# Causal attention with one exp over a pair of key blocks instead of one exp for each

## The reference

```python
x = x + _layernorm(_L0_attn_ref(_layernorm(x), Wq, bq, Wk, bk, Wv, bv, Wo, bo))
x = x + _layernorm(_L0_ffn_ref(_layernorm(x), w_up, w_down))
...
scores = jnp.einsum('bqhd,bkhd->bhqk', Q, K)
causal = jnp.tril(jnp.ones((S, S), bool))
scores = jnp.where(causal[None, None], scores, -jnp.inf)
attn = jax.nn.softmax(scores.astype(jnp.float32), axis=-1).astype(X.dtype)
out = jnp.einsum('bhqk,bkhd->bqhd', attn, V).reshape(B, S, D)
return out @ Wo.T + bo
```

## Time and profile before

| | |
|---|---|
| two runs, median | 6665.75 us (6662.55 and 6668.95) |
| the profiled execution, its own time | 6643.92 us |
| its span on core 7, first to last instruction | 6642.4 us |
| spans of the eight cores | 6576.3 to 6642.4 us |
| PE busy | 3147.3 us (47 %), 10388 matmuls |
| ACT busy | 907.2 us (14 %) |
| DVE busy | 1902.5 us (29 %) |
| mean granted PE clock, core 7 | 0.704 of full speed |

### The profile page before, as it was taken

How to read it: one execution, slowest core, us unless ns; L and a number is a source line. 1 busy time by engine, 2 the same in 40 slices (tenths; PEclk the granted TensorE clock), 3 DMA queues, 4 the chain that set the end, 5 groups by cost and what they waited for, 6 DMA issues and landing times.

```text
span 6642.4 us, 35789 instructions; the slowest of 8 cores (6576.3 to 6642.4 us)
## 1 busy us (share of the span) xinstructions
PE 3147.3 (47%) x10388; PEld 1086.2 (16%) x10388; DVE 1902.5 (29%) x2752; ACT 907.2 (14%) x1249; POOL 380.4 (6%) x716
## 2 busy tenths in 40 slices
PE   0000744444744445554446544443857636566276
PEld 0000311111211111211112110111323212222132
DVE  1153121111111111211111311113456265263562
ACT  1100001112011111022111012220011111011110
POOL 0001100000100000100001000001000000000000
PEclk9999855555755556655557655555878868788688
DMA  5677210000200001200001100013133334433343
GB/s 95 101 253 209 44 38 31 32 31 32 45 25 32 31 32 34 60 16 24 29 32 42 41 32 32 19 73 127 51 103 104 95 120 108 152 101 96 108 118 98
DMA packets 358610, 472.21 MB, mean 71 GB/s; under 512 B 161553, under 2 KB 317201, under 8 KB 337681
## 3 DMA queue, kind: packets, MB, share of 16 engines
q0 software_dynamic: 69136, 251.74, 13.6%
q1 hardware_dynamic: 289282, 218.19, 12.3%
HBM read 385.92 MB, written 83.89 MB: 71 GB/s over the span
## 4 chain that ended last, share of the span: by engine, by line
PE 40%; DVE 17%; DMA 15%; ACT 13%; issue 6%; DVEq 4%; POOL 2%; SPq 2%; ACTq 0%; POOLq 0%
ACT pt L643 7%; PE psB L660 6%; PE psB L1033 6%; PE psB L1159 5%; PE psA L634 4%; PE psB L664 4%; PE psB L435 3%; PE psB L473 3%; PE psB L559 3%; DMA xt<-x 3%; DMA wqch<-wdnt 3%; DMA wqch<-wupt 2%; PE psB L776 2%; DVE tq_bf L387 2%; PE psB L505 2%
## 5 line engine op out<-in xcount | busy, mean ns | idle before, releaser
L660 PE MATMUL psB<-pt,ones_bf 128*128 128x512 bf16 x640 | 374.1, 585 | 789.6 <-DVEq L91 431.7
L1033 PE MATMUL psB<-wsl_f,qfm_ar 128*128 128x512 bf16 x2048 | 476.4, 397 | 434.2 <-DMA qfm_ar<-qtile 434.2
L1159 PE MATMUL psB<-wsl_f,qfm_ar 128*128 128x512 bf16 x2048 | 503.6, 412 | 268.8 <-DMA qfm_ar<-qtile 221.4
L643 ACT ACTIVATE pt<-psA,negC 128x512 bf16<-128x512 f32 x640 | 439.7, 687 | 1134.7 <-PE psA L634 1132.7
L650 DVE TENSOR_TENSOR pt<-pt,strip 128x512 bf16<-128x512 bf16 x256 | 109.0, 426 | 1474.0 <-ACT pt L643 1474.0
L634 PE MATMUL psA<-qh,kg 128*128 128x512 bf16 x640 | 397.9, 622 | 83.9 <-ACTq L91 83.9
L664 PE MATMUL psB<-pt,vg 128*128 128x512 bf16 x640 | 404.3, 632 | 0.0
L585 PE MATMUL psB<-sq_t,ones_f 128*128 128x512 f32 x128 | 87.3, 770 | 565.7 <-DVEq L91 565.7
L559 PE MATMUL psB<-y_fm,wsl 128*128 128x512 bf16 x1024 | 288.0, 444 | 134.8 <-DVEq L91 134.8
L1033 PEld LDWEIGHTS psB<-wsl_f,qfm_ar 128*128 128x128 bf16 x2048 | 206.6, 101 | 704.0 <-issue 484.4
L435 PE MATMUL psB<-y_fm,wsl 128*128 128x512 bf16 x1024 | 231.0, 390 | 180.9 <-DVEq L91 124.5
(11 more groups left out here) (153 smaller groups left out, 3013.2 us busy)
## 6 DMA issues: line engine op xcount, KB each, us to landing
wsl_f<-tup_sp SPq DMA_DIRECT2D x512, 128.0 KB, 2.8
wsl_f<-tdn_sp SPq DMA_DIRECT2D x512, 128.0 KB, 2.9
wch<-wupt POOLq DMA_DIRECT2D x16, 2048.0 KB, 8.7
wch<-wdnt POOLq DMA_DIRECT2D x32, 1024.0 KB, 5.4
wqch<-wupt POOLq DMA_DIRECT2D x32, 1024.0 KB, 5.7
wqch<-wdnt POOLq DMA_DIRECT2D x32, 1024.0 KB, 5.9
xt<-x SPq DMA_DIRECT2D x16, 1024.0 KB, 12.4
tup_sp<-tq_bf POOLq DMA_DIRECT2D x128, 128.0 KB, 2.2
```

The costliest lines, as they stand in the source:

```text
L643: exp_done[(hq, k)] = p.op("scalar", lambda e, sl=sl: e.activation(out=p4(sl), in_=S4[sl][:, :], func=ACT.Exp, bias=negC[:], scale=1.0), i ...
L660: p.op("tensor", lambda e, sl=sl, k=k, nk=nk: e.matmul(PS[5][:, :], ones_bf[:, :], p4(sl), start=(k == 0), stop=(k == nk - 1)))
L1033: t_mm = p.op("tensor", lambda e, par=par, c=c, t=t, j=j: e.matmul(PS[par][:, :], q1fm[:, c * 512 + t * 128: c * 512 + (t + 1) * 128], wsl ...
L1159: t_mm = p.op("tensor", lambda e, par=par, c=c, t=t, s=s: e.matmul(PS[par][:, :], q2fm[:, c * 512 + t * 128: c * 512 + (t + 1) * 128], wsl ...
```

## The change

Key blocks are handled in pairs: `u` counts pairs, `ns = nk // 2` is their number, `sb = u % 2` the buffer. For a pair PE issues two score matmuls (after: L632, L636) into the two halves of one 1024-column slot of `psA`; only the second raises the semaphore. ACT computes one exp over the 1024 columns (L645). In a masked pair DVE applies two masks, one to each half (L655), and signals once. PE then issues two row-sum matmuls (L666, L669) and two value matmuls (L672, L677). The keys of `exp_done`, `mask_done` and `pv_mm` are pairs now, so the waits two slots back go by pairs. As `nk - 4` is even, a pair is masked in both halves or in none. The line numbers of the code behind the loop are 13 higher.

```diff
-                for k in range(nk):
-                    sl = k % 4
-                    if k >= 4:
-                        p.wait("tensor", SA, exp_done[(hq, k - 4)])
-                    elif hq >= 1:
-                        p.wait("tensor", SA, exp_done[(hq - 1, nk_prev - 4 + k)])
...
-                    t_smm = p.op("tensor", lambda e, sl=sl, hl=hl, k=k, qsl=qsl: e.matmul(
-                        S4[sl][:, :],
-                        kg[:, hl * S + k * 128: hl * S + (k + 1) * 128],
+                for u in range(ns):
+                    sb = u % 2
+                    if u >= 2:
+                        p.wait("tensor", SA, exp_done[(hq, u - 2)])
+                    elif hq >= 1 and ns_prev - 2 + sb >= 0:
+                        p.wait("tensor", SA, exp_done[(hq - 1, ns_prev - 2 + sb)])
...
+                    p.op("tensor", lambda e, sb=sb, hl=hl, u=u, qsl=qsl: e.matmul(
+                        S2[sb][:, 0:512],
+                        kg[:, hl * S + (2 * u) * 128: hl * S + (2 * u + 1) * 128],
+                        qsl, start=True, stop=True))
+                    t_smm = p.op("tensor", lambda e, sb=sb, hl=hl, u=u, qsl=qsl: e.matmul(
+                        S2[sb][:, 512:1024],
+                        kg[:, hl * S + (2 * u + 1) * 128: hl * S + (2 * u + 2) * 128],
                         qsl, start=True, stop=True), inc=ST)
                     p.wait("scalar", ST, t_smm)
...
-                    exp_done[(hq, k)] = p.op("scalar", lambda e, sl=sl: e.activation(
-                        out=p4(sl), in_=S4[sl][:, :], func=ACT.Exp,
+                    exp_done[(hq, u)] = p.op("scalar", lambda e, sb=sb: e.activation(
+                        out=p_t[sb][:], in_=S2[sb][:, 0:1024], func=ACT.Exp,
                         bias=negC[:], scale=1.0), inc=SA)
...
+                        for half in range(2):
+                            kc = 2 * u + half
+                            if kc >= nk - 4:
+                                m = kc - 4 * qb
+                                p.op("vector", lambda e, sb=sb, m=m, half=half: e.tensor_tensor(
+                                    out=p_t[sb][:, half * 512:(half + 1) * 512],
+                                    in0=p_t[sb][:, half * 512:(half + 1) * 512],
+                                    in1=strip[:, 384 - 128 * m: 896 - 128 * m],
+                                    op=ALU.mult))
+                        mask_done[(hq, u)] = p.sig("vector", SV)
+                    p.wait("tensor", SA, exp_done[(hq, u)])
                     if diag:
-                        p.wait("tensor", SV, mask_done[(hq, k)])
-                    if k == 0 and qb == 0:
+                        p.wait("tensor", SV, mask_done[(hq, u)])
+                    if u == 0 and qb == 0:
                         p.wait("tensor", SV, cap_v)
```

More of the change, by code:

```diff
@@ L655, in build_core @@
-                    p.wait("tensor", SA, exp_done[(hq, k)])
+                        p.wait("vector", SA, exp_done[(hq, u)])
+                        for half in range(2):
[7 more added lines that the diff above has]
+                                    op=ALU.mult))
@@ L663, in build_core @@
-                    pv_mm[(hq, k)] = p.op("tensor",
-                        lambda e, sl=sl, k=k, qpar=qpar, hl=hl, nk=nk: e.matmul(
+                    p.op("tensor", lambda e, sb=sb, u=u: e.matmul(
+                        PS[5][:, :], ones_bf[:, :], p_t[sb][:, 0:512],
+                        start=(u == 0), stop=False))
+                    p.op("tensor", lambda e, sb=sb, u=u, ns=ns: e.matmul(
+                        PS[5][:, :], ones_bf[:, :], p_t[sb][:, 512:1024],
+                        start=False, stop=(u == ns - 1)))
@@ L665, in build_core @@
+                    p.op("tensor", lambda e, sb=sb, u=u, qpar=qpar, hl=hl: e.matmul(
+                        PS[6 + qpar][:, :],
+                        vg[:, (2 * u) * 512 + hl * 128: (2 * u) * 512 + (hl + 1) * 128],
+                        p_t[sb][:, 0:512], start=(u == 0), stop=False))
+                    pv_mm[(hq, u)] = p.op("tensor",
+                        lambda e, sb=sb, u=u, qpar=qpar, hl=hl, ns=ns: e.matmul(
                             PS[6 + qpar][:, :],
-                            vg[:, k * 512 + hl * 128: k * 512 + (hl + 1) * 128],
@@ L667, in build_core @@
-                            p4(sl), start=(k == 0), stop=(k == nk - 1)),
+                            vg[:, (2 * u + 1) * 512 + hl * 128: (2 * u + 1) * 512 + (hl + 1) * 128],
+                            p_t[sb][:, 512:1024], start=False, stop=(u == ns - 1)),
                         inc=ST)
-                p.wait("scalar", ST, pv_mm[(hq, nk - 1)])
+                p.wait("scalar", ST, pv_mm[(hq, ns - 1)])
                 if hq >= 2:
```

29 lines of the change are left out of this document (9 added, 20 removed).

## The result

The changed kernel took 6206.98 us (median of 11 runs, 6198 to 6253), the kernel before 6662.32 us (10 runs). The ratio is 0.9324, with a 95 % interval of 0.9301 to 0.9347: 455 us less, where 250 were forecast. The direction was right, the size was not. A twelfth run of the changed kernel, not in that median, took 6252 us.

The account below looks back on a forecast made before the run. The attention's serial chain of engines taking turns was taken as the bound. Savings of 127 us (unmasked pairs), 116 (masked) and 7 (head starts) total 250: 6665.75 - 250 = 6416 us, range 6375 to 6480.

Parts of the forecast that it names:

- The serial chain: Attention loop: engines take turns, nothing overlaps, quantization waits behind it; blocks of 2.37 us unmasked, 2.98 masked.
- The estimate of the wide exp: Attention's 1024-column exp: about 280 ns plus 0.833 ns a column, 1133 ns; the prediction itself took 1.12 us.
- The sum of 250 us: Attention saving: unmasked pairs 127 us, masked pairs 116, head starts 7, all at 1.2 GHz.
- the granted clock of the attention: PE's clock in the attention, held at 1.2 GHz throughout the sum; forecast chance 0.87.
- that rival: PE's clock rises to 2.4 GHz in the attention: 6174 us for all unmasked pairs, 6295 for half; chance 0.07.
- The reading of the busy share: In the attention, streamed columns fill 63 % of PE's time in place of 54 %: denser, but no row shows a rise.
- a slow exp: Attention's wide exp pays a width penalty: 6538 us at 1.5 us each; chance 0.04 together with a chain elsewhere.
- a chain that goes elsewhere: Prefetched weights for the next group come late, so the program stays at 6666 us; chance 0.04 together with slow exp.

Follow-up runs that it names:

- pair_broken_long: Changed kernel with each next pair's score matmuls held until ACT saw the previous value matmuls end and ran two small activations; 6631 us, ratio 0.996.
- single_plus2: Kernel before with the score matmul of every key block issued three times, five matmuls a block; 7167 us, ratio 1.078.
- pair_exp_twice: Changed kernel with the wide exp computed twice, a drain between, the six matmuls kept together; 6745 us, ratio 1.012.

## Why the prediction was wrong

- **The serial chain, its links at a given clock and its exposure: right.** Pair 4.07 us (4.08 forecast), masked 5.02 (5.05), wide exp 1.114 (1.12), the two masks 0.76 (0.78), 438 of 439 us on core 7 between its first and last exp. The estimate of the wide exp by the Trainium skill (ScalarE: Activation LUTs, What ACT_TABLE_LOAD costs), 1133 ns, was 19 ns too high; the trace has 1114.
- **The sum of 250 us: nearly right, and not all.** pair_broken_long gives 277 us for the structure at 1.2 GHz. The remaining 178 to 205 us of the 455 are put down to the clock. The same from the rows: the row-sum matmul's mean fell from 585 to 478 ns, (585 - 478) / (585 - 380) = 52 % of the pairs at the full clock, x 320 x 1.26 us = 210 us, an estimate (core 3 is one of the cores with the least clock in the attention).
- **The step that failed is the granted clock of the attention, held at 1.2 GHz in the sum and given a chance of 0.07 to rise.** The runs showed 0.72 to 0.78 in the unmasked pairs, where the sum has 0.50. "No row shows a rise after work with gaps like these" was true, and was taken as evidence against the rise. But the kernel before has next to no stretch like these: its attention has groups of three matmuls, its projections unbroken runs of 16 and more, and by its trace on core 7 there is a single run of bf16 matmuls between the two lengths (eight of L776). The rows could not tell, and the change moved PE from the one towards the other. Its price was worked out well (2.82 us a pair, 6174 for all and 6295 for half of the unmasked pairs); but only the unmasked pairs were priced, and the masked ones held the clock as well (3.76 in place of 5.02 us, 0.80 to 0.85 on average), which is how the result could come so near to the full price with half the clock. That 6207 lies so near to 6174 is chance: a part of the clock in the unmasked pairs and a part in the masked ones happen to add up to it.
- **The range** left out both times of that rival. It had been stretched by 15 us for a mechanism worth up to 242. The chances add up to 0.94 for faster by over 2 %, where 0.93 is given; nothing hangs on it.
- **The reading of the busy share** was the wrong gauge in itself: 63 % against 54 % looked like a small step, and single_plus2 with 66 % and a clock of 0.50 shows that the average share does not decide.
- The Trainium skill (TensorE: Matmul & The Clock Gate, What's actually happening) has the full clock released by activity. Here that speaks for the rival that came true, and the trace now agrees beyond unbroken runs: the rise came in groups of six with 1.36 us of idle time between them (the L666 row of the timeline).
- The rivals with a slow exp, and with a chain that goes elsewhere, did not happen: the exp has no penalty for reading 1024 columns.

What stays open: why six close matmuls and not five. The runs give the count for bf16 matmuls of 512 columns with these pauses, no more. One more point was already in the trace of the kernel before: the f32 matmuls of the key norm come in twos.

```profile
834.21 2.05 PE L505 MATMUL psB<-sq_t,ones_f 128*128 128x512 f32 x2 [2.23 <-DVEq L91]
```

PE is busy with them for 2.05 us of each 4.28, 48 %, nearly the share of pair_exp_twice, and from 830 to 860 the granted clock was 0.50 throughout: the same average share without the group of six, and no rise.

That the clock rises at another place from head to head (a head's 20 exps took 74 to 86 us from first to last by the trace) was seen and not explained.

## What to carry to other kernels

In a serial loop at 1.2 GHz, moving matmuls together can be worth more than the waits it saves, since it may bring the clock; price each link at both clocks and give the second price a real chance whenever the trace has no stretch of the new kind. Less work for PE can cost time: look at which clock a saving leaves behind (five matmuls a pair took 6233 us, six 6207). And where two engines take turns, the larger gain is in the order of the instructions: issuing the next scores ahead of the wait brought another 579 us (6207 to 5628) with the same instructions.

## What the runs showed of the hardware that was not expected

- The clock of TensorE rose to 2.4 GHz in stretches filled to only 49 %, when the matmuls stood in groups of six, and stayed at 1.2 GHz in all 384 unmasked blocks a core filled to 66 % in groups of five.
- A pause of 0.27 us inside the group costs part of the clock (0.57 to 0.65 in the unmasked pairs, against 0.72 to 0.78), one of 0.82 us all of it (0.50).
- Once up, the clock held through masked pairs of 3.76 us with six matmuls each, but with pauses of some 2.5 us (pair_exp_twice) it fell again within a few pairs.
- Two activations with no wait between them overlap: the second exp began 0.58 us after the first, which is listed with 0.69. Two masks on DVE took 0.76 for 2 x 0.42.
- The clock record has a third level besides 0.50 and 1.00. In the profiled execution of the changed kernel cores 0 to 3 have 456 to 587 us each at 0.81, cores 4 to 7 none; 23 to 121 us of it lie inside the attention's pairs. The same stretch on core 0 and on core 4, both in an unbroken run of matmuls (76 against 94 in 20 us):

```profile
1560.00:1580.00 20.00, 19.82 (x76) 8.31 (x77) 3.46 (x5) 0.00 (x0) 0.00 (x0) 0.81 0.00 1
1560.00:1580.00 20.00, 20.00 (x94) 9.04 (x93) 4.15 (x6) 0.00 (x0) 0.00 (x0) 1.00 0.00 0
```

What brings it about is open. The figures of core 3 above come from an execution with it, and cores 0 to 3 have the lower end of the changed kernel's clock in the table (0.72 to 0.74, against 0.74 to 0.78 on cores 4 to 7).
